# Values of the second attention stage in four parts of eight heads, their weights in the shared buffer, longer strips of exponentials, and shifted start times in both attention stages

## What is computed

```python
x = x + 0.5 * L0_ffn(layernorm(x))
x = x + L0_attn(layernorm(x))      # 16 heads of 32, 4 key/value heads, rope, biases
x = x + 0.5 * L0_ffn(layernorm(x))
x = x + 0.5 * L1_ffn(layernorm(x))
x = x + L1_attn(layernorm(x))      # 16 heads of 32, no biases; the stage of this change
x = x + 0.5 * L1_ffn(layernorm(x))

def L1_attn(x):
    q, k, v = split(x @ w_attn)                     # each (2, 1024, 512)
    att = softmax(causal(q @ k.T / sqrt(32)))       # for each of 16 heads
    return (att @ v) @ w_proj
```

## Time and profile before

| | |
|---|---|
| median of 3 runs | 2652.11 us (2651.18 to 2652.96) |
| the profiled execution | 2646.1 us, its span 2644.4 us |
| PE busy | 2543.7 us (96%) |
| DVE, ACT, POOL busy | 56%, 40%, 37% |
| mean granted TensorE clock | 0.990 |
| first attention (units) | about 344 to 786 us |
| second attention (units) | 1630.5 to 2096 us |

### The profile page before, as it was taken

The page is one execution under the profiler, slowest core; times in us unless marked ns, Lnnn a source line. Parts: engine busy times, 40 slices in busy tenths (PEclk is TensorE's granted clock), DMA queues, the critical chain, the costliest instruction groups (busy, mean ns, idle before and its releaser), DMA issues.

```text
span 2644.4 us, 43617 instructions
## 1 busy us (share of the span) xinstructions
PE 2543.7 (96%) x16928; PEld 2016.4 (76%) x16928; DVE 1472.0 (56%) x2780; ACT 1045.2 (40%) x1901; POOL 969.1 (37%) x1357
## 2 busy tenths in 40 slices
PE   6999989899999999999999999999999899999999
PEld 4788867667668888888888878776777678888887
DVE  7777578878875445433333345787578643333333
ACT  7555346655653223311111133566456532211111
POOL 3333566666653335211111122666366521111110
PEclk9999989999999999999999999999999999999999
DMA  4222131122130110100000002333132100000001
GB/s 148 72 72 72 38 76 45 47 65 65 45 100 0 37 44 9 41 25 24 24 24 25 24 16 57 90 93 77 45 94 68 47 33 24 24 24 25 24 16 64
DMA packets 71997, 128.69 MB, mean 49 GB/s; under 512 B 15728, under 2 KB 24944, under 8 KB 71792
## 3 DMA queue, kind: packets, MB, share of 16 engines
q1 hardware_dynamic: 71792, 125.92, 16.6%
HBM read 62.42 MB, written 13.63 MB: 29 GB/s over the span
## 4 chain that ended last, share of the span: by engine, by line
PE 81%; DVE 6%; POOL 3%; ACT 3%; issue 2%; SPq 2%; DMA 1%; DVEq 0%; ACTq 0%; POOLq 0%
PE psum L1018 66%; PE psum L1103 4%; PE psum L1140 4%; PE psum L1121 4%; PE psum L1151 2%; DVE psum L1472 2%; SPq L1697 1%; PE psum L1027 1%; SPq L1716 1%; POOL rstd L1575 1%; POOL s4a1e L1623 1%; POOL s1a0e L1623 1%; ACT s1a0e L1306 1%; DVE stats L1338 0%; ACT s4a1e L1306 0%
## 5 line engine op out<-in xcount | busy, mean ns | idle before, releaser
L1472 DVE CUSTOM_DVE_ANT_0 psum<-psum,mask_q 128x512 f32<-128x512 f32 (+7 forms) x512 | 385.5, 766 | 170.4 <-PE psum L1103 168.4
L1018 PE MATMUL psum<-hA_hi,wmem 128*128 128x256 f32 (+1 forms) x1536 | 405.2, 334 | 0.9 <-ACT s4a1e L1306 0.8
L1018 PEld LDWEIGHTS psum<-hA_hi,wmem 128*128 128x128 f32 x1536 | 270.2, 190 | 31.9 <-ACT s4a1e L1306 1.4
L1018 PE MATMUL psum<-hA_lo,wmem 128*128 128x512 f32 (+1 forms) x864 | 293.5, 340 | 0.0
L1306 ACT ACTIVATE s4a1e<-psum,p_scale 128x384 f32<-128x384 f32 (+5 forms) x384 | 204.9, 580 | 82.7 <-PE psum L1121 80.3
L1306 ACT ACTIVATE s1a0e<-psum,p_scale 128x384 f32<-128x384 f32 (+5 forms) x384 | 201.6, 579 | 73.2 <-PE psum L1121 72.6
L1425 DVE SCALAR_TENSOR_TENSOR x<-psum,x 128x512 f32<-128x512 f32 x256 | 175.8, 689 | 97.3 <-PE psum L1018 93.8
L1396 DVE TENSOR_TENSOR s5f1prod<-psum,s5f1silu 128x512 f32<-128x512 f32 x64 | 44.3, 692 | 302.0 <-PE psum L1018 302.0
L1396 DVE TENSOR_TENSOR s3f1prod<-psum,s3f1silu 128x512 f32<-128x512 f32 x64 | 44.3, 692 | 294.1 <-PE psum L1018 294.1
L1587 POOL TENSOR_TENSOR wmem<-raw,wmem 128x512 fp32r<-128x512 f32 x58 | 74.3, 1291 | 326.1 <-ACT wmem L1208 326.1
L1018 PE MATMUL psum<-s3f1w,s3f1a 128*128 128x512 f32 x768 | 181.6, 390 | 0.9 <-POOL s3f1w L1587 0.9
(11 more groups left out here) (192 smaller groups left out, 5515.2 us busy)
## 6 DMA issues: line engine op xcount, KB each, us to landing
s1a0qst<-s1a0qs SPq DMA_DIRECT2D x96, 128.0 KB, 2.4
s4a1qst<-s4a1qs SPq DMA_DIRECT2D x96, 128.0 KB, 2.5
s4a1kst<-s4a1ks SPq DMA_DIRECT2D x96, 128.0 KB, 2.4
raw<-in_gate SPq DMA_DIRECT2D x44, 256.0 KB, 2.8
raw<-in_up SPq DMA_DIRECT2D x44, 256.0 KB, 2.8
raw<-in_down SPq DMA_DIRECT2D x44, 256.0 KB, 2.8
rounded<-s0f0w SPq DMA_DIRECT2D x24, 256.0 KB, 2.0
s2f0w<-rounded SPq DMA_DIRECT2D x24, 256.0 KB, 5.0
```

Source lines behind the costliest of these rows:

```text
L1018: ins = pe.matmul(out_, w, m, start=n == 0, stop=n == len(terms) - 1)
L1472: dve.tensor_tensor_reduce(scores, scores, mask_q[:, SEQ - width:SEQ].rearrange("p (z w) -> p z w", z=scores.shape[1]), -1.0, -MASKED, ALU ...
```

## The change

1. Stage a1's values are computed in four parts, of one batch and eight heads each: a tile is 12 matmuls of 256 columns, and there are 32 tiles. The part of the first eight heads stands in front of the heads as before. The others start in groups 1, 3 and 5, at units 14, 16 to 28.
2. Their weights are two pieces a part and share `wmem`: half 0 holds q and k of one group, half 1 the value weights. A group's q and k weights are written once the pieces of the group before have been computed. The value weights of parts 1 to 3 are loaded at units 4 and 6 of groups 1, 3 and 5. The q and k weights of group 1, which were loaded at the end of the stage before, are now loaded behind the 24 stack DMAs of group 0, and the `vw` buffer is gone.
3. The ring of exponentials grows to 11264 columns in a0 and 11776 in a1.
4. In both attention stages: `y_fin` and `y_move` one unit later, the gap to `y_hi` one shorter (it stays at unit 14), the first `oproj` one unit later (18); q and k weights at units 17 and 19 in place of 20 and 22; output weights at 27 in place of 23.

```diff
-Y_AT = 1
+Y_AT = 2
-YT_AT = 2
-O_LAG = 1
-QK_W_AT = 20
-O_W_AT = 23
+YT_AT = 1
+O_LAG = 2
+QK_W_AT = 17
+O_W_AT = 27
-PV_LAG = 9
+PV_LAG = {"a0": 9, "a1": 9}
+PV_BY = {"a0": 2, "a1": 2}
+V_AT = 14
+V_STEP = 2
+V_W_AT = 4
-E32 = 7680
+E32 = {"a0": 11264, "a1": 11776}
+HALVES, VH = 2, 8
...
+    def v_weights_of(s, vp):
+        return [split(s, "v", vp, i) for i in range(2)]
...
-        return group_weights(s, 0) + group_weights(s, 1)
+        return group_weights(s, 0) + (group_weights(s, 1) if STAGES[s] == "a0" else
+                                      v_weights_of(s, 0))
...
-        v_weights.waiting += [split(s, "v", 0, k) for k in range(1 if grouped else KT)]
+        v_weights.waiting += [split(s, "v", 0, 0)] if grouped else []
...
         side = Beside(plan)
+        if not grouped:
+            for job in group_weights(s, 1):
+                side.start(job)
         side.waiting += values(0)
...
-            put(values(1), HEADS * ST + (PV_LAG + 1) // 2 * 2 - 8, 1)
+            for vp in range(1, BATCH * HALVES):
+                put(v_weights_of(s, vp), (2 * vp - 1) * UNITS + V_W_AT, 2)
+                put(values(vp), (2 * vp - 1) * UNITS + V_AT, V_STEP)
...
             if name in "qk":
-                return [wmem[:, g % 2, 2 * "qk".index(name) + p, :] for p in range(2)]
+                slot = g % 2 if STAGES[s] == "a0" else 0
+                return [wmem[:, slot, 2 * "qk".index(name) + p, :] for p in range(2)]
             if name == "v":
-                return [q[:, i, :] for q in T[s]["vw"]]
+                return [wmem[:, 1, 2 * p + i, :] for p in range(2)] if STAGES[s] == "a1" else \
+                    [q[:] for q in T[s]["vw"]]
...
-                products(ps[:, 0, :], [(hA[hp][:, k, t * P:(t + 1) * P], vw[wp][:, k, :])
+                products(ps[:, 0, 0:VH * HD],
+                         [(hA[hp][:, k, t * P:(t + 1) * P], vw[wp][:, k, :])
```

More of the change, by code:

```diff
@@ L345, in attention @@
             behind.append((n, i))
-            if len(behind) > PV_LAG and i % 2 == 1:
-                times_v(*behind.pop(0))
-                times_v(*behind.pop(0))
+            if len(behind) > pv_lag and i % pv_by == pv_by - 1:
+                for _ in range(pv_by):
+                    times_v(*behind.pop(0))
             for job in beside.pop(u, []):
@@ L521, in run @@
         elif kind == "v_tile":
-            done[step] = work("pe", 2.8, *banks)
+            done[step] = work("pe", 1.4, *banks)
         elif kind == "v_chunk":
@@ L602, in bank_turns, with strip_turns @@
     return banks, earlier
-def strip_turns(plan, size):
+def strip_turns(plan, sizes):
     place, before, at = {}, {}, defaultdict(int)
@@ L614, in strip_turns @@
         width = SEQ - unit[2] * P
-        begin = at[key] if at[key] + width <= size else 0
+        begin = at[key] if at[key] + width <= sizes[STAGES[key]] else 0
         at[key] = end = begin + width
@@ L746, in build @@
                     t["qst"] = sbuf(sc, f"{tag}qst", [P, HPG, SEQ], F32R)
-                    vp = 1 if kind == "a0" else KT
-                    t["vw"] = [sbuf(sc, f"{tag}vw{p}", [P, vp, D], F32R) for p in range(2)]
                     if kind == "a0":
+                        t["vw"] = [sbuf(sc, f"{tag}vw{p}", [P, D], F32R) for p in range(2)]
                         t["rope"] = {n: sbuf(sc, f"{tag}rope{n}", [P, SEQ]) for n in "qk"}
@@ L870, in w_ready @@
                 return sem["w_lo"], at("w_lo", "w_split", s, name, g, i)
-            i = KT - 1 if name == "v" and STAGES[s] == "a1" else 0
+            i = 1 if name == "v" and STAGES[s] == "a1" else 0
             return sem["w_lo"], at("w_lo", "w_split", s, name, g, i)
@@ L980, in head_of, with v_of, v_before @@
             return (HPG * j + g, j, j) if STAGES[s] == "a0" else (n % HEADS, j, n % HEADS)
-        def v_of(s, jt):
-            return jt // CT if STAGES[s] == "a0" else jt
+        def v_of(s, n, jt):
+            return (n // HEADS, jt // CT) if STAGES[s] == "a0" else (n // VH, jt)
         def v_parts(s, b, t):
[L987 to L991, removed]
+            first, n = (0, KV0) if STAGES[s] == "a0" else (b % HALVES * VH, VH)
+            tiles = slice(t * CT, (t + 1) * CT) if n == KV0 else slice(t, t + 1)
+            fill = (("v_turn", s, b, t), "v_tp") if n == KV0 else (("v_tile", s, b, t), "v_mm")
+            cols = (tiles.stop - tiles.start) * n * HD
+            src = psum[:, banks[fill[0]][0], 0:cols].rearrange("p (t h d) -> p t h d", h=n, d=HD)
+            return fill, tiles, src, T[s]["v"][:, :, first:first + n, :]
+        def v_before(s, b, tile):
+            ahead, heads = (1, HEADS) if STAGES[s] == "a0" else (HALVES, VH)
+            return (sem["pv"], at("pv", "pv", s, (b - ahead + 1) * heads - 1, tile)) \
+                if b >= ahead else None
         def halves(ps, width):
```

53 lines of the change are left out of this document (31 added, 22 removed).

## The result

The changed kernel takes 2662.7 us (median of 6 runs, 2656.7 to 2665.4) against 2652.5 for the kernel before on the same chip: ratio 1.0033, 95% interval 1.0018 to 1.0048. It is slower by some 9 to 10 us where 4 us of gain were forecast, and the time lies just above the range. The profiled execution is the slowest of the six. One execution of the kernel before, 2997.4 us at a mean granted clock of 0.791, is left out of every comparison here.

What follows compares the result with a forecast made beforehand. PE was taken to bound the kernel, busy 96% of the span. Heads' PE work +12.3 and front +4.0 against -20.3 for the rest gave -4.0 us, from 2652.1 to 2648 us; range 2632 to 2661.

Steps and rivals of the forecast that it cites:

- The front: Before the second attention's heads: group 1's weights wait behind 24 stack DMAs; first key step at 1634.5, +4.0 us.
- PE's work: Value tiles of 1.43 us, weight loads hidden: 10.6 us less PE work before second attention's heads, 12.3 more beside them.
- the gains of the start times: Both attentions: moved starts end waits, -5.5, -4.0, -1.2 and -2.7, with -6.8 for the clock: -20.2 us.
- Weights at 17: Both attentions: earlier q and k weight loads end ACT's waits and PE's idles behind them: -5.5 and -4.0 us.
- Finish, products and output weights: Both attentions: output weights' split avoids products, -1.2; PE's waits on y_lo go, -2.7; later finish costs under 1 us.
- The clock: PE's half-clock stretches at 381 and 1924 go, the one at 1668 halves: -6.8 us, bounds 0 and -9.
- New waits of the tiles: Second attention: 24 value tiles need banks and evictions, value weights queue late: +1.5 us, bounds 0 and 12.
- The -1.6 for a stack: Second attention, group 3: the last k stack stops holding PE, two value tiles standing ahead of it: -1.6 us.
- The front costs nothing: Before the heads: ACT passes both splits before PE runs short; first key step 10.6 us earlier, 2633; chance 0.22.
- The tiles cost a wait each: Second attention, units 17 to 28: each of 24 tiles costs a wait; at 0.5 us +12, 2660; chance 0.22.
- The clock stays low: Before the heads: PE's 10 us of work after the stall run at half rate, +9, 2657; chance 0.06.
- the two signs of being wrong: First key step at 1620, or PE's idle in the second attention's units not below 21.8 us.

Runs made afterwards that it cites:

- x_front: The kernel after with group 1's q and k weights planned ahead of the second attention's 24 stack DMAs: 2649.1 us, ratio 0.9993 to the kernel before.
- x_fvalues: x_front with all five old start times (values beside the heads, shared buffer and long ring alone): 2642.2 us, ratio 0.9962 to the kernel before.
- x_values: The kernel after with all five old start times, its front unrepaired: 2658.5 us, ratio 1.0026 to the kernel before.
- x_times: The kernel before with all five new start times in both attentions and nothing else: 2649.9 us, ratio 0.9996.
- x_qk17: The kernel before with q and k weights started at unit 17 instead of 20 and nothing else: 2645.3 us, ratio 0.9977.
- x_same: The kernel before, unchanged, profiled once more: 2656.8 us.
- x_yo: The kernel before with later finish, output products one unit later and output weights at 27, q and k weights still at 20: 2659.8 us, ratio 1.0042.
- x_w: The kernel before with q and k weights loaded from unit 17 and output weights from unit 27, nothing else: 2680.7 us, ratio 1.0115.
- the repair by penalty: x_front and x_fvalues, each with a bank of the row step just before counted free 1.0 us later for row steps: ratios 1.0002 and 1.0041.
- the two pairs here: x_front and x_fvalues, each compared with itself plus the bank-dealing penalty: 2650.4 us against 2649.1, and 2659.3 against 2642.2.

## Why the prediction was wrong, by its own steps

**The front: right, in every link.** Taken back by the 9 us by which all of it is later: both splits end at 1620.9 (forecast 1621.2 to 1621.9), behind 17.4 us of DMA wait (over 10); PE stops at 1610.5 (1611) for 11.15 us (11); the first key step, at 1643.87, comes at 1634.8 (1634.5). From the first attention's end it comes 5.7 us later than before (4.0 forecast); with the stall gone the same stretch is 13.8 us shorter (861.0 to 847.2). In whole times the stall is worth 13.6 us by medians and 10.6 by the ratios with the new start times (x_front), 16.3 and 17 with the old ones (x_fvalues against x_values), forecast 14.6. Its clock was undersized. A stretch of the kernel after, columns as in the earlier trace rows:

```profile
1622.20:1635.90 13.70, 5.19 (x20) 4.91 (x21) 3.30 (x7) 1.80 (x4) 2.50 (x2) 0.50 0.44 111
```

and value tiles of it in the chain that ended last:

```profile
1632.47 2.56 PE psum L1046 x12
1636.06 1.43 PE psum L1046 x12
```

The granted clock is at its lower level, 1.2 GHz, from 2.6 us after PE stopped until 5.2 us after it started again, and the first value tile then takes 2.56 us in place of 1.43. 5.2 us at half rate lose 2.6, against 1.5 assumed. The Trainium skill (page "TensorE: Matmul & The Clock Gate", section on what is actually happening) says that the throttled state is the default and activity releases it; the rows agree.

**PE's work: somewhat too large.** A new tile takes 1.43 us, as a piece did. The stretch up to the heads holds 8.9 us less PE work in x_front than before (forecast 10.6), and the second attention's units 8.8 more in x_front than in x_times (452.2 against 443.4; forecast 12.3). The 214 ns a matmul that an unhidden weight load would have given did not appear.

**The failed step: the gains of the start times.** The prediction added -5.5 and -4.0 for the weights at 17, -1.2 for the output weights, -2.7 for the products and -6.8 for the clock, whose stretches it tied to the waits on weights: -20.2 us. x_times has just these times and measured -0.8 us (0.9996). Each wait of ACT that was named did vanish; in x_times none for q or k is left of the 14.2 us, and PE's waits on exponentials fell as told. The error was to book the idle time that stood behind a vanished wait as a gain: 8.8 us of waits on exponentials went, and 11.2 us of waits on row maxima came. The idle time of PE over both attentions is 53.5 us in x_times and was 50.7 and 54.0 in the two profiles of the kernel before.

Two sub-steps can be told apart. Weights at 17: -9.5 forecast, and -16.3 with the clock that hung on them; -6 measured by itself (x_qk17). The sign is right, but the path is not shown: ACT waits less for k, and little of it reaches PE's waits on exponentials (at the key steps, both attentions, 0.2 us less than in the rows, 1.7 less than in x_same). PE's idle time is 1 to 5 us less, and the clock of its runs (0.9906 against 0.9888), at 1.8 us for 0.001, goes with 3 us. Finish, products and output weights: -3.9 forecast, +10 measured (x_yo). There the sentence that failed is "`y_fin` one unit later passes only a 128-column row maximum on DVE (0.3 us) ... under 1 us in all". It followed the moved step in the queues, and did not ask what bank each step would have. "No new wait" for the output weights at 27 was true only because the finish moved with them; x_w paid 36 us more than x_qk17 for that coupling, which the prediction didn't see.

**The clock.** The three stretches at 0.5 that were to go were taken for consequences of three idle stretches. The mean granted clock of x_times did rise, from 0.9888 to 0.9902. At 1.8 us for 0.001 that is 2.5 us, not 6.8; so its waits may have cost a little more than before, not less. Read in slices of 1 us, its profile has no stretch at 0.5 any more at 381 and at 1924, but the one at 1668, forecast to halve, still lasts 6.8 us (from 1674), and three of the first attention, from 468, 540 and 701, last 6.6 to 6.8. In all it is 53.5 us at the lower level, against 53.9 and 70.8 in the two profiles of the kernel before: others took the place of those that went.

**New waits of the tiles: wrong side.** +1.5 were assumed, bounds 0 and 12. With old start times the values beside the heads gained 9 to 10 us (x_fvalues) where the prediction's terms for them, with a free front, make 12.3 - 10.6 + 1.5 - 1.6 = +1.6. Some 2.5 us of that are clock (0.9902 against 0.9888); PE's idle time in the second attention's units fell from 21.8 and 23.6 us to 17.7, in which more work covers the same waits. With the new start times they gain nothing (x_front against x_times, 0.7 us), so this gain and that of the weights at 17 look like the same idle time, filled twice. That is argued from the table, not shown. The -1.6 for a stack came in part: PE's waits on k stacks in the second attention are 2.1 us in the kernel after, 2.7 before. With the stall the terms of the values make +16.2; x_values measured +7 to 8. So this error, of some 9 us, hid about half of the one in the start times: that the time came only 2 us above the range is luck.

**The rivals.** "The front costs nothing" did not happen; x_front, where it is made to happen, is 2649, not 2633, for the start times' gain was missing. "The tiles cost a wait each" gave the nearest time, 2660, by a cause that is refuted: x_fvalues has the tiles and gains. "The clock stays low" was half right: 5.2 us of work at the lower level, not 10 us. In steps by the ratios the kernel after is -1 (x_times), -1 (the values on top of it, x_front) and +10.6 (the stall): these are differences between the same runs, so their sum has to be the measured +9 and shows nothing more.

**The signs.** Neither of the two signs of being wrong came: the first key step was not at 1620, and PE's idle in the units of the second attention is 17.2 us, below 21.8. Both look at the second attention; in the first, where half of the start times' gain was to come, PE's idle was not below the old one (31.3 us, against 28.9 and 30.4).

**The base.** The sum was put on an execution that lay 6 us below the median; two profiles of one kernel are 10.6 us apart, and waits of the sizes summed here (0.4 to 2.7 us) are smaller than what one profile can tell. That widened no term in the prediction, and should have.

**Left open.** Why the three times of finish, products and output weights cost some 10 us. Banks are dealt otherwise with them, the waits on row maxima are the visible difference, and dealing alone can move 17 us. Their lower clock (x_yo 0.9870 against 0.9888) goes with some 3 us of it, as cause or as consequence. But the repair by penalty did not recover the loss, so whether it is the banks that lose it, is not shown.

## What to carry to other kernels

A load that is planned behind a burst of DMA issues on the same queue is late by the whole burst: sum the issue times of the queue ahead of it (24 issues, 15.4 us here), and plan it ahead of the burst. A vanished wait is a gain only as far as the engine has nothing else to wait for within that time; where several resources are nearly short (exponentials, row maxima, banks), take a part of it and test the terms one by one, for two that are each worth 6 to 10 us may be worth nothing together. Where banks are dealt by a planner, any moved step deals them anew: the two pairs here moved by 1 and by 17 us.

## What was not expected of the hardware

TensorE's granted clock is not a property of the kernel alone. In the runs of the unchanged kernel that are compared its mean lay between 0.985 and 0.993, with times from 2660 down to 2640 us; the means over the runs of one kernel still differed between kernels (0.9846 in x_w to 0.9906), so it has to be compared over many runs. And the longest stretch at half clock in the kernel after, 13.7 us, began 2.6 us into one stop of PE of 11.15 us, and outlasted it by 5.2 us of work.
